# Where the residual sum runs: x added to the output rows by VectorE instead of GpSimd

## The reference

```python
xn = _layernorm(x, axis=-1)
s = _L0_attn_ref(xn, ...)     # conv + residual, minGRU + residual, GELU feed-forward + residual
g = _silu(_L0_ffn_ref(xn, L0_ffn_w_gate, L0_ffn_w_up, L0_ffn_w_down))
x = x + s * g

# in _L0_attn_ref
x = causal_dwconv(rmsnorm(x, conv_norm_g), ...) + x
x = min_gru(rmsnorm(x, gru_norm_g), gru_w) + x
h = gelu(rmsnorm(x, ff_norm_g) @ ff_w1.T + ff_b1)
x = h @ ff_w2.T + ff_b2 + x

# in _L0_ffn_ref; fp4_linear quantises both operands to FP4 in blocks of 16
h = silu(fp4_linear(x, w_gate)) * fp4_linear(x, w_up)
return fp4_linear(h, w_down)
```

## Time and profile before

| | us |
|---|---|
| median of 3 runs | 1054.61 |
| profiled execution, its device time | 1054.15 |
| its span | 1052.4 |
| PE busy | 1035.2 |
| DVE busy | 973.6 |
| ACT busy | 627.8 |
| GpSimd busy | 123.1 |
| GpSimd, the 15 sums of L762 | 36.1 |

### The profile page before, as it was taken

How to read it: one execution, slowest core, us unless ns; L and a number is a source line. 1 busy time by engine, 2 the same in 40 slices (tenths; PEclk the granted TensorE clock), 3 DMA queues, 4 the chain that set the end, 5 groups by cost and what they waited for, 6 DMA issues and landing times.

```text
span 1052.4 us, 18459 instructions
## 1 busy us (share of the span) xinstructions
PE 1035.2 (98%) x6884; PEld 964.1 (92%) x6884; DVE 973.6 (93%) x1883; ACT 627.8 (60%) x1010; POOL 123.1 (12%) x116
## 2 busy tenths in 40 slices
PE   6999999999999999999999999999999999999998
PEld 5689989999899999989999898999989999998998
DVE  6899999999999999999999999999999999999886
ACT  4776374565746557484655838456574745757452
POOL 1010211011011100111110011101101110111000
PEclk9999999999999999999999999999999999999999
DMA  7000010010101001020010101001010200101001
GB/s 255 1 21 1 2 61 1 21 41 9 53 1 57 5 21 41 2 61 1 30 33 21 41 1 61 1 21 40 22 40 1 61 1 21 41 2 40 2 1 60
DMA packets 29382, 31.45 MB, mean 30 GB/s; under 512 B 1136, under 2 KB 28528, under 8 KB 29296
## 3 DMA queue, kind: packets, MB, share of 16 engines
q1 hardware_dynamic: 28192, 29.17, 9.0%
q10 hardware_dynamic: 1104, 1.13, 0.3%
HBM read 21.90 MB, written 8.39 MB: 29 GB/s over the span
## 4 chain that ended last, share of the span: by engine, by line
PE 93%; DVE 4%; DMA 1%; ACT 1%; issue 1%; ACTq 0%; POOL 0%; DVEq 0%
PE gu_ps L1075 48%; PE w_ps L1075 30%; PE w_ps L1149 4%; PE gu_ps L1087 1%; PE w_ps L1087 1%; PE w_ps L1098 1%; PE w_ps L1198 1%; DMA w_f<-pw_t_dram 1%; PE gu_ps L1133 1%; PE gu_ps L1141 1%; PE w_ps L1161 1%; PE w_ps L1141 1%; PE w_ps L1160 1%; PE w_ps L1133 1%; PE w_ps L1241 0%
## 5 line engine op out<-in xcount | busy, mean ns | idle before, releaser
L1075 PE MATMUL gu_ps<-gu_hi,xq_hi 128*128 128x352 f32 x512 | 167.8, 328 | 0.2 <-ACT act L898 0.2
L1075 PE MATMUL gu_ps<-gu_lo,xq_hi 128*128 128x352 f32 x512 | 165.7, 324 | 0.0
L1075 PE MATMUL gu_ps<-gu_hi,xq_lo 128*128 128x352 f32 x512 | 165.4, 323 | 0.0
L1075 PE MATMUL w_ps<-w_hi,act_hi 128*128 128x256 f32 x480 | 138.8, 289 | 0.2 <-DVE act_lo L486 0.2
L1075 PE MATMUL w_ps<-w_hi,act_lo 128*128 128x256 f32 x480 | 135.2, 282 | 0.0
L1075 PE MATMUL w_ps<-w_lo,act_hi 128*128 128x256 f32 x480 | 134.9, 281 | 0.0
L755 POOL TENSOR_TENSOR inv_rms<-ss_row,neg_half 128x4 f32<-128x4 f32 x32 | 35.8, 1119 | 684.5 <-DVE ss_row L509 684.5
L1075 PE MATMUL gu_ps<-xs_hi,w_hi 128*128 128x512 f32 x256 | 101.3, 396 | 1.3 <-DVE xs_lo L523 1.3
L1075 PE MATMUL gu_ps<-xs_hi,w_lo 128*128 128x512 f32 x256 | 101.0, 394 | 0.0
L1075 PE MATMUL gu_ps<-xs_lo,w_hi 128*128 128x512 f32 x256 | 100.9, 394 | 0.0
L1075 PEld LDWEIGHTS gu_ps<-gu_hi,xq_hi 128*128 128x128 f32 x512 | 96.3, 188 | 0.6 <-issue 0.4
(11 more groups left out here) (156 smaller groups left out, 2702.4 us busy)
## 6 DMA issues: line engine op xcount, KB each, us to landing
x_res<-x_dram SPq DMA_DIRECT2D x16, 512.0 KB, 4.7
x_in<-x_dram SPq DMA_DIRECT2D x15, 512.0 KB, 4.0
out_dram<-o SPq DMA_DIRECT2D x15, 512.0 KB, 3.2
act<-w_t_dram SPq DMA_DIRECT2D x1, 1024.0 KB, 12.0
w_f<-w_t_dram SPq DMA_DIRECT2D x1, 1024.0 KB, 14.4
w_f<-w_down_dram SPq DMA_DIRECT2D x1, 704.0 KB, 10.1
hid<-w_gate_dram SPq DMA_DIRECT2D x1, 640.0 KB, 5.9
hid<-w_up_dram SPq DMA_DIRECT2D x1, 640.0 KB, 8.0
```

What stands on the lines that cost most here:

```text
L1075: done = M.matmul(psum, l, r, start=first and i == 0, stop=last and i == len(terms) - 1)
```

## The change

The function `output_sum` moves from GpSimd to DVE. GpSimd's operation and its three waits go, and `taps_next`, which held the number of the DVE step, goes with them. On DVE the sum stands behind `front_fp4_low(c + 1)` and ahead of `front_stats(c + 2)`; in body 15, which has no front, it is the last call. It waits for sg_ready, which DVE raises itself, and for xres_ready.

```diff
+            def output_sum(c):
+
+                dve.wait_ge(sg_ready, T * (c + 1))
+                dve.wait_ge(xres_ready, 16 * (c + 1))
+                V.tensor_tensor(o[:], o[:], x_res[:], ALU.add).then_inc(out_ready, 1)
...
                 if front:
                     ratios = front_fp4_ratios(c + 1)
-                    taps_next[c + 1] = ratios
...
                     front_fp4_low(c + 1)
+                    output_sum(c - 1)
                     if c + 2 < B:
                         carried["stats"] = front_stats(c + 2)
+                else:
+                    output_sum(c - 1)
...
-            def output_sum(c):
-
-                pool.wait_ge(sg_ready, T * (c + 1))
-                pool.wait_ge(*((dve_step, taps_next[c + 2]) if c < B - 2 else (actlo_ready, KF * B)))
-                pool.wait_ge(xres_ready, 16 * (c + 1))
-                nc.gpsimd.tensor_tensor(o[:], o[:], x_res[:], ALU.add).then_inc(out_ready, 1)
...
                 rms_scale(c * 2 + 1)
-                output_sum(c - 1)
```

More of the change, by code:

```diff
@@ L256, in mixed_recurrent_kernel @@
         block = ctx.enter_context(nc.Block())
-        taps_next = {}
         halves = lambda w: w[:].rearrange("p (a k) n -> p a (k n)", a=KD)
```

## The result

The changed kernel takes 1058.89 us (median of 5, 1058.69 to 1059.68) against 1054.61 before (median of 5 by now): ratio 1.0046, 95% interval 1.0035 to 1.0056. By the two medians it is slower by 4.3 us; the ratio makes it 4.8, and against the 1054.07 and 1054.16 that the kernel before gave beside the experiments it is 4.8 and 4.7. The forecast was 1061.8, slower by 7.2. The profiled execution took 1058.84 (span 1057.1), 4.69 more than the one before.

The account below looks back on a forecast made before the run. PE was taken to set the pace; each chunk grows by 1.14 - 0.55 - 0.04 = 0.55 us, 13 times 7.15, plus 0.3 on 1054.15 makes 1061.6, given as 1061.8; range for 8 of 10: 1057.8 to 1064.5.

Parts of the forecast that it names:

- DVE's slot: Sum on DVE: start of the sum to start of its independent successor L400, taken as 1.14 us.
- The number of chunks: Sums of bodies 1 to 13 push bodies 2 to 14, 13 times; body 15's DVE waits of 1.49 swallow 1.14.
- its own account: Whole chain of soaked waits and PE push: 0.55 us growth per chunk, 1061.8 us, range 1060 to 1063.5, chance 0.73.
- the second rival: DVE alone sets the growth, as one engine's balance: 0.37 us per chunk, chunks of 62.67, 1059.0 us; chance 0.10.
- The first L493 soaks 0.26, the second 0.30: DVE's two waits before L493 in a chunk absorb lateness from 1.14, leaving 0.58 us late.
- L517: DVE operation late in the chunk, whose wait of a few hundredths soaks 0.04 us of lateness.
- all of it, 0.54, at L1141: PE's weight load behind GpSimd's power has 0.04 us of room, so 0.58 of lateness pushes PE by 0.54.
- hid's product: PE's gate product needing hid (L470), early in the chunk: at most 0.2 us of push, not added to the later one.
- the waits of PE for GpSimd's scale and for L502: Sign of being right: together about 0.55 us per chunk in bodies 2 to 14, none in 15.
- signs of being wrong: Chunks of 62.3 with PE never waiting, chunks of 62.67, or PE held first at hid's product.
- A statement about L457: DVE's 0.18 us wait ahead of L457 soaks no more as ScalarE moves with PE, yet was to be gone.
- The allowance of 0.3 for accidents: Late starts such as 0.46 before L382, soaked by slack before the change: 0 to 0.6 us for two, 0.3 taken.

Follow-up runs that it names:

- e1: Changed kernel with the DVE sum adding x to only one column of each tile, place, waits and store kept: 1054.44 us.
- e6: Changed kernel with the DVE sum over two of the four tiles only, at the same place: 1054.27 us.
- e3: Changed kernel with the DVE sum over three of the four tiles, at the same place: 1055.51 us.
- e4: Changed kernel with the whole DVE sum 18 us later in the order, behind hidden_low of tile 2 in the next body, behind both hqt_lo waits: 1070.65 us.
- e5: Changed kernel with the whole DVE sum 7 us earlier in the order, behind the quantised rows and ahead of y_lo: 1063.29 us.
- e7: Changed kernel with the whole DVE sum between the two hqt_lo waits, behind hidden_low of tile 1 in the next body: 1062.87 us.

## Why the prediction came out as it did

**The direction was right, and the mechanism in the main.** DVE's slot, the two soaking waits, a push at L1138 and the room lost for good are in the trace. e1 shows the removed GpSimd operation and the moved store at zero, as forecast. The slot was forecast as 1.14 and is 1.13. The number of chunks was right: body 15 swallowed its sum, and its end adds nothing (from xq of chunk 15 to the end of the span, 90.24 us before and 90.23 after). The measured time lies in the range of 1057.8 to 1064.5, but below the 1060 to 1063.5 that the prediction gave to its own account: the wider range holds it because it took in the second rival's 1059.0.

**The size was too large by 2.9 us, and one term did it.** "The first L493 soaks 0.26, the second 0.30" took what is printed between the end of one operation and the start of the next. But had they waited for nothing, these two operations would have started 0.09 before their predecessors' printed ends, as they do after the change and as 1.14 against 1.23 in the very row used for the slot let one expect. The slot was counted from start to start and the waits from end to start. Counted alike, the two waits soak 0.36 each, and L517 soaks 0.08 instead of 0.04. The growth is 1.13 - 0.72 - 0.08 = 0.33, and 13 times that is 4.3, against the 7.15 forecast: the term that was mis-sized is what DVE's waits soak, 0.55 + 0.04 forecast and 0.80 measured. e6 and e3 bear it out, with no loss at a slot of 0.60 and 0.05 at 0.87.

**The push is not at one handover.** The prediction put all of it, 0.54, at L1141, since the larger hold was to cover the smaller. The loads show 0.14 there, 0.15 earlier at hid's product and 0.03 at L1130, and the waits of PE for GpSimd's scale and for L502, forecast as 0.55 a chunk, aren't there: the waits view has nothing for L1138 and 1.7 us in two times for L1130. Two of the prediction's own signs of being wrong are there: the chunk of 62.62 us is nearer to the 62.67 of the second rival than to 62.85, and PE is held first at hid's product. The second rival falls on other evidence, given below; the hold at hid's product, forecast as at most 0.2, is there 13 times (2.5 us), and it is part of the 0.33 instead of being covered by a larger hold.

**A statement about L457 contradicted its own argument.** The prediction had ScalarE move with PE, which leaves the wait ahead of y_lo as it is; yet it said that this wait would be gone. It is there 13 times, with its 0.18. The argument was right and the sign to look for was wrong.

**The rival that DVE alone sets the growth** gave 0.37 per chunk and 1059.0 us, which is close to the measured time. It is nevertheless not what happens. It counts the wait ahead of y_lo as used up, and that is still there. With waits counted rightly it would give 1.13 - 0.72 - 0.27 - 0.08 = 0.06. e4, e5 and e7, which have the same DVE work and growths of 1.17, 0.60 and 0.65, exclude that DVE's total sets it. That its number came out right is luck: two errors, one of size and one of mechanism, met there.

**The allowance of 0.3 for accidents** was fair in kind: in the profiled execution after, one chunk grew by 0.6 more than its neighbours, behind another late start of 0.46. With the chunks starting 0.28 earlier it accounts for nearly all of the distance from 4.3 to the 4.69 of the two profiled executions.

## What to carry to other kernels

Room is measured start to start: compare the distance of two starts where nothing waits with the distance where something does, and don't read it off the idle time between them, which here understated 0.36 as 0.27. How far an operation overlaps with the one ahead differs by the pair (0.09 at most places here, nothing at L514), so take it from the pair in question. To place added work, follow it to the first handover to the engine that sets the pace; waits ahead of the work don't help, and the sum of an engine's idle time isn't the measure (the same DVE work cost 4.7, 8.7, 9.1 and 16.6 us by its place). Work that fits at no single place may fit in pieces at two (4.7 or 9.1 us in one piece, 1.8 in two).

## What the runs showed of the hardware

The two-input f32 addition in SBUF took 426 ns for 256 columns, 680 for 512 (e6), 949 for 768 (e3) and 1216 for 1024: 0.25 to 0.27 us for each 256. GpSimd's sum of 2.41 us ran beside DVE's taps 14 times and left them at 741 to 746 ns (L442), as where no sum runs. The last sum of the kernel before, at 1029.01, took 2.39 us beside L493 (0.82) and L356 (0.89), which take the same elsewhere. It never ran beside a DVE operation that reads two tensors from SBUF. A push of PE by 0.1 to 0.2 us can appear in no total of waits: the hold at L1138 (0.14) has no row, the one at hid's product has one of the weight loads alone, and in the changed kernel the chunks grow by 0.33 while PE is busy for 62.62 of 62.62 us.
